# A token table built in setup: its numbers are written out earlier, the own tiles' are gathered first, and the setup's products, mixes and prefills take another order

## Time and profile before

| | us |
|---|---|
| median of 3 runs | 1506.09 |
| lowest, highest | 1505.55, 1506.47 |
| the profiled execution, its own time | 1516.0 |
| its span, first to last instruction | 1514.3 |
| PE busy | 1465.3 (97%) |
| DVE, ACT, POOL busy | 1047.0, 1146.8, 959.1 |
| mean granted clock of PE | 0.997 |

### The profile page before, as it was taken

The page is one execution under the profiler, slowest core; times in us unless marked ns, Lnnn a source line. Parts: engine busy times, 40 slices in busy tenths (PEclk is TensorE's granted clock), DMA queues, the critical chain, the costliest instruction groups (busy, mean ns, idle before and its releaser), DMA issues. The chain is left out here.

```text
span 1514.3 us, 33889 instructions
## 1 busy us (share of the span) xinstructions
PE 1465.3 (97%) x11160; PEld 1339.9 (88%) x11160; DVE 1047.0 (69%) x2811; ACT 1146.8 (76%) x3477; POOL 959.1 (63%) x991
## 2 busy tenths in 40 slices
PE   5789999999999999999999999988999999999999
PEld 2469888888888988889888898877999999999999
DVE  7887788788777887778887787763344333356665
ACT  5589888888888888888888888865555555555555
POOL 7175567888788888788878877664677566510000
PEclk9999999999999999999999999999999999999999
DMA  7324511211211111111111111022244234456665
GB/s 237 132 73 163 164 38 49 69 48 42 60 38 39 55 42 36 35 56 34 36 56 34 37 38 48 26 60 67 69 116 106 70 71 109 120 158 190 189 184 146
DMA packets 171503, 126.48 MB, mean 84 GB/s; under 512 B 30309, under 2 KB 154959, under 8 KB 171330
## 3 DMA queue, kind: packets, MB, share of 16 engines
q1 hardware_dynamic: 153794, 104.15, 23.3%
q0 software_dynamic: 17536, 20.17, 4.8%
HBM read 61.64 MB, written 78.66 MB: 93 GB/s over the span
## 5 line engine op out<-in xcount | busy, mean ns | idle before, releaser
L1129 ACT ACTIVATE expd<-masked,nmax 128x128 f32<-128x128 f32 x1024 | 396.0, 393 | 0.3 <-DVE nmax L1282 0.3
L925 POOL TENSOR_TENSOR prob<-expd,rtotal 128x1024 f32<-128x1024 f32 x128 | 243.5, 1902 | 117.3 <-DVE rtotal L1251 115.8
L1265 DVE COPY_PREDICATED masked<-off_diag,ps_s 128x1024 f32<-128x1024 int32 x128 | 175.0, 1367 | 164.3 <-PE ps_s L1018 164.3
L1062 PE MATMUL ps_o<-u,probT 128*128 128x128 f32 x2048 | 249.0, 275 | 0.0
L1062 PEld LDWEIGHTS ps_o<-u,probT 128*128 128x128 f32 x2048 | 238.9, 191 | 0.0
L1129 ACT ACTIVATION_READ_ACCUMULATOR expd<-masked,nmax 128x1 f32 x1024 | 197.0, 192 | 0.0
L1138 ACT ACTIVATE u<-ps_ut 128x1024 f32<-128x1024 f32 x128 | 131.4, 1026 | 66.3 <-PE ps_ut L1073 66.3
L1227 DVE TENSOR_TENSOR w_lo<-ps_w,w_hi 128x512 fp32r<-128x512 f32 x256 | 164.3, 681 | 0.9 <-ACT w_hi L1167 0.9
L1167 ACT ACTIVATE w_hi<-ps_w 128x512 fp32r<-128x512 f32 x256 | 146.1, 595 | 15.7 <-PE ps_w L1048 9.3
L1158 ACT ACTIVATE probT<-ps_ut 128x1024 f32<-128x1024 f32 x128 | 131.4, 1027 | 33.9 <-PE ps_ut L1030 27.5
L1046 PE MATMUL ps_w<-xT_hi,M_hi 128*128 128x256 f32 x512 | 154.1, 301 | 3.0 <-DVE xT_lo L1221 2.2
(11 more groups left out here) (261 smaller groups left out, 3824.9 us busy)
## 6 DMA issues: line engine op xcount, KB each, us to landing
turned<-x2T SPq DMA_DIRECT2D x32, 256.0 KB, 2.2
answers_sp<-zeros SPq DMA_DIRECT2D x16, 512.0 KB, 4.3
answers_fq<-zeros SPq DMA_DIRECT2D x16, 512.0 KB, 3.8
xT<-turned SPq DMA_DIRECT2D x56, 128.0 KB, 2.3
sh_back<-answers_sp SPq DMA_DIRECT2D x56, 128.0 KB, 2.4
sh_back<-answers_fq SPq DMA_DIRECT2D x56, 128.0 KB, 2.5
out<-res SPq DMA_DIRECT2D x56, 128.0 KB, 2.1
h_sb<-in_L_tok_weight SPq DMA_DIRECT2D x12, 512.0 KB, 5.9
```

The costliest lines, as they stand in the source:

```text
L925: nc.gpsimd.tensor_tensor(prob[k % 2][:, :].rearrange("p (g j) -> p g j", g=H), expd[k % 2][:, :].rearrange("p (g j) -> p g j", g=H), rtot ...
L1062: mm = nc.tensor.matmul(ps_o[:, 0:D], probT[k % 2][:, g * N:(g + 1) * N], u[k % 2][:, g * D:(g + 1) * D], start=(g == 0), stop=(g == H - 1))
L1129: ins = nc.scalar.activation(expd[(k - 1) % 2][:, g * N:(g + 1) * N], masked[(k - 1) % 2][:, g * N:(g + 1) * N], ACT.Exp, bias=nmax[(k - 1 ...
L1265: nc.vector.copy_predicated(masked[k % 2][:, :].rearrange("p (g j) -> p g j", g=H), off_diag[:, :].unsqueeze(1).to_broadcast([P, H, N]), p ...
```

## The change

- DVE writes the plain numbers (not the thousandths) and the flags into `numbers` early, the flags in the middle of `thousandths`, which now runs once over all 98 columns; the thousandths go to `part`. SP writes `kept` right after the small loads, **ahead** of the three weight loads and the rows, after a wait for the numbers and the flags.
- The four number gathers stand on POOL ahead of `head_of`'s masks, and the four row gathers behind them: two after the masks, two after the ten small memsets, all ahead of the mixes.
- The gathered numbers are plain, so DVE makes their thousandths at c == 5 (8 more small operations).
- `turn_b` is made by POOL (8 operations) in place of DVE.
- PE does the first turn and the coefficients at c == 3 (before c == 2), the other turns at 4 and 5, the products from c == 6 on, the last two at c == 12.
- The prefills go from ACT to POOL, right behind the mixes.
- `WARM` goes from 13 to 6.

The diff, cut to its core:

```diff
--- before.py
+++ after.py
@@ -56,7 +56,7 @@
 AHEAD = 2
-WARM = 13
+WARM = 6
 CLEARS = B * N // P // CLEAR_ROWS
...
@@ -296,7 +296,7 @@
-        part = sb("part", [P, 4, VS])
+        part = sb("part", [P, 3, VX])
@@ -378,16 +378,28 @@
...
             made["own"] = link.n
+            link.inc(nc.gpsimd.tensor_scalar(turn_b, row_f[:, :], TURN_HI, 0.0, ALU.mult, ALU.add))
+            link.inc(nc.gpsimd.tensor_scalar(turn_lo, row_f[:, :], TURN_LO, 0.0, ALU.mult, ALU.add))
+            link(nc.gpsimd.tensor_scalar(turn_hi.bitcast(F32R), row_f[:, :], TURN_HI, 0.0, ALU.mult, ALU.add))
+            link(nc.gpsimd.tensor_tensor(turn_b, turn_b, turn_hi, ALU.subtract))
+            link(nc.gpsimd.tensor_tensor(turn_lo, turn_lo, turn_b, ALU.add))
+            link(nc.gpsimd.tensor_tensor(turn_b, turn_hi, turn_lo, ALU.subtract))
+            pool.wait_ge(S["link"], 1)
+            link(nc.gpsimd.tensor_tensor(turn_b, turn_b, is_hi[:, :].to_broadcast([KR, D]), ALU.mult))
+            nc.gpsimd.tensor_tensor(turn_b, turn_b, turn_lo, ALU.add).then_inc(S["turn"], 1)
             def own_number(t):
...
                                              bass.IndirectOffsetOnAxis(ap=ids0[:, t:t + 1], axis=0)).then_inc(S["numbers0"], 16)
-            pool.wait_ge(S["ids0"], 16)
-            for t in range(OWN):
+            def own_row(t):
                 nc.gpsimd.indirect_dma_start(h_sb[:, (VS + t) * D:(VS + t + 1) * D], None, weight,
                                              bass.IndirectOffsetOnAxis(ap=ids0[:, t:t + 1], axis=0)).then_inc(S["rows0"], 16)
+            pool.wait_ge(S["ids0"], 16)
+            pool.wait_ge(S["kept"], 32)
+            for t in range(OWN):
+                own_number(t)
             link.inc(nc.gpsimd.memset(head_of[:, :], 1.0))
...
@@ -404,18 +416,22 @@
...
                                         mix_co[:, c % HC, c // HC, :].unsqueeze(2).to_broadcast([P, H, D]), ALU.mult).then_inc(S["mixed"], 1)
-            pool.wait_ge(S["kept"], 32)
-            for t in range(OWN):
-                own_number(t)
-            pool.wait_ge(S["coef_out"], 2)
-            pool.wait_ge(S["wT_out"], 1)
-            for c in range(2 * HC):
-                mix(c)
+            for t in range(2):
+                own_row(t)
             for t, value in ((C.power, -0.5), (C.ones, 1.0), (C.tri, 1.0), (C.carry, 0.0), (C.chosen, 0.0), (C.var, 1.0)):
...
             made["mv1"] = link.n
+            for t in range(2, OWN):
+                own_row(t)
+            pool.wait_ge(S["coef_out"], 2)
+            pool.wait_ge(S["wT_out"], 1)
+            for c in range(2 * HC):
+                mix(c)
+            for k in range(2):
+                link.inc(nc.gpsimd.tensor_copy(masked[k][:, :].rearrange("p (g j) -> p g j", g=H),
+                                               diag[:, :].unsqueeze(2).to_broadcast([P, H, N])))
             link.inc(nc.gpsimd.iota(C.rank_i[:, :], [[-1, E]], base=E, channel_multiplier=0))
...
@@ -443,14 +459,14 @@
...
                 sp.dma_start(dst, src, allow_slow_non_contiguous=True).then_inc(S["small"], 16)
+            sp.wait_ge(S["numbers"], 2)
+            sp.dma_start(kept[0:P * VR, :].rearrange("(p r) c -> p (r c)", p=P),
+                         numbers[:, 0:VR, :].rearrange("p r c -> p (r c)")).then_inc(S["kept"], 16)
+            sp.dma_start(kept[P * VR:VOCAB, :], numbers[0:REST, VR, :]).then_inc(S["kept"], 16)
             for dst, src in ((wq[:, :], Wq), (wkv[:, :], Wkv),
...
             sp.dma_start(h_sb[:, cols(0)], w_main[:, cols(0)]).then_inc(s_row[0], 16)
-            sp.wait_ge(S["numbers"], 1)
-            sp.dma_start(kept[0:P * VR, :].rearrange("(p r) c -> p (r c)", p=P),
-                         numbers[:, 0:VR, :].rearrange("p r c -> p (r c)")).then_inc(S["kept"], 16)
-            sp.dma_start(kept[P * VR:VOCAB, :], numbers[0:REST, VR, :]).then_inc(S["kept"], 16)
             one = slice((CHUNKS - 1) * CH, VR * D)
...
@@ -499,10 +515,6 @@
...
                 nc.scalar.activation(turns[c % 2][:, 0:w], ps_a[c % 2][:, 0:w], ACT.Copy).then_inc(S["whole"], 1)
-            def prefill(k):
-                nc.scalar.activation(masked[k][:, :].rearrange("p (g j) -> p g j", g=H),
-                                     diag[:, :].unsqueeze(2).to_broadcast([P, H, N]), ACT.Copy).then_inc(S["coef_out"], 1)
             def sines(c):
...
@@ -522,7 +534,7 @@
...
                     rest_of_numbers()
-                if c == 2:
+                if c == 3:
                     act.wait_ge(S["wT"], 1)
...
@@ -532,15 +544,10 @@
...
                     nc.scalar.activation((wkT, wvT)[c - 4][:, :, :].rearrange("p c n -> p (c n)"), ps_t[:, :], ACT.Copy).then_inc(S["wT_out"], 1)
-                if c == 4:
-                    act.wait_ge(S["coef_out"], 2)
-                    prefill(0)
                 if c == 6:
...
                     nc.scalar.activation(numT[:, 12 * P:13 * P], short_rows, ACT.Copy).then_inc(S["numT_out"], 1)
-                if c == CHUNKS - 2:
-                    prefill(1)
-                if c == 9:
+                if c == 10:
                     act.wait_ge(S["M"], 2)
...
@@ -606,73 +613,61 @@
...
             angles(1)
-            pe.wait_ge(S["num_f"], 2)
             for c in range(4, CHUNKS - 1):
...
                 angles(c)
-                if c == 2:
+                if c == 3:
                     turn(0)
                     coefficients()
-                if c in (3, 4):
-                    turn(c - 2)
+                if c in (4, 5):
+                    turn(c - 3)
                 if c == 6:
-                    pe.wait_ge(S["num_f"], 3)
+                    pe.wait_ge(S["num_f"], 2)
                     number_rows(CHUNKS - 1).then_inc(S["numT"], 1)
-                if 5 <= c:
+                for n in {6: (0,), 7: (1,), 8: (2,), 9: (3,), 10: (4,), 11: (5,), 12: (6, 7)}.get(c, ()):
                     for half in range(2):
-                        product((c - 5) // HC, (c - 5) % HC, half)
+                        product(n // HC, n % HC, half)
             pe.wait_ge(S["reduced"], CHUNKS - 1)
...
         def _(dve):
-            link = Chain(dve, sem("s_link"))
-            def thousandths(at):
-                value, q, hi, lo = (part[:, n, at] for n in range(4))
-                link(nc.vector.tensor_copy(value, num_i[:, at]))
+            link = Chain(dve, S["link"])
+            def thousandths(at, flags=False):
+                value, (q, hi, lo) = numbers[:, at, 0], (part[:, n, at] for n in range(3))
                 link(nc.vector.tensor_scalar(q, value, 0.001, None, ALU.mult))
...
                 link(nc.vector.tensor_tensor(hi, hi, lo, ALU.subtract))
+                if flags:
+                    dve.wait_ge(S["isn"], 32)
+                    nc.vector.tensor_copy(numbers[:, 0:VR, 1].bitcast(I32), isn[:, 0:VR]).then_inc(S["numbers"], 1)
+                    nc.vector.tensor_copy(numbers[:, VR:VS, 1].bitcast(I32), rest_isn[:, 0:1]).then_inc(S["numbers"], 1)
                 link(nc.vector.tensor_tensor(lo, q, hi, ALU.subtract))
...
                 link(nc.vector.scalar_tensor_tensor(lo, lo, -1000.0, hi, ALU.mult, ALU.add))
-                link(nc.vector.scalar_tensor_tensor(numbers[:, at, 0], lo, 0.001, q, ALU.mult, ALU.add))
+                link(nc.vector.scalar_tensor_tensor(q, lo, 0.001, q, ALU.mult, ALU.add))
             def halves(chunks, n):
-                src = numbers[:, chunks.start * VC:chunks.start * VC + (chunks.stop - chunks.start) * n, 0].rearrange("p (c r) -> p c r", r=n)
-                for part in (0, 2):
-                    link.inc(nc.vector.tensor_copy(num_hl[:, chunks, 0:n, part], src))
-                link.wait()
-                for part in (0, 2):
-                    ins = nc.vector.tensor_tensor(num_hl[:, chunks, 0:n, part + 1], src, num_hl[:, chunks, 0:n, part].bitcast(F32), ALU.subtract)
-                ins.then_inc(S["num_f"], 1)
+                src = part[:, 0, chunks.start * VC:chunks.start * VC + (chunks.stop - chunks.start) * n].rearrange("p (c r) -> p c r", r=n)
+                high, low = (num_hl[:, chunks, 0:n, k:PARTS:2] for k in range(2))
+                both = src.unsqueeze(3).to_broadcast([P, chunks.stop - chunks.start, n, 2])
+                link(nc.vector.tensor_copy(high, both))
+                nc.vector.tensor_tensor(low, both, high.bitcast(F32), ALU.subtract).then_inc(S["num_f"], 1)
             dve.wait_ge(S["made"], made["own"])
             link.inc(nc.vector.tensor_reduce(is_hi[:, :], own_hi[:, :], X_AXIS, ALU.max))
-            link.inc(nc.vector.tensor_scalar(turn_b, row_f[:, :], TURN_HI, None, ALU.mult))
-            link(nc.vector.tensor_scalar(turn_hi.bitcast(F32R), row_f[:, :], TURN_HI, None, ALU.mult))
-            link(nc.vector.tensor_tensor(turn_b, turn_b, turn_hi, ALU.subtract))
-            link(nc.vector.scalar_tensor_tensor(turn_lo, row_f[:, :], TURN_LO, turn_b, ALU.mult, ALU.add))
-            link(nc.vector.tensor_tensor(turn_b, turn_hi, turn_lo, ALU.subtract))
```

(17 more changed lines are left out.)

## The result

The kernel after takes **1522.46 us** (median of 4 runs, 1521.57 to 1523.46) where the kernel before took 1505.82 beside it (4 runs, 1504.11 to 1506.47): ratio 1.0112 [1.0095, 1.0130], slower by 16.6 us. The forecast, 1510.2, had the sign, and its range ended at 1514.5. The profiled execution of after took 1521.61 us, 1519.9 of them the span.

What follows compares the result with a forecast made beforehand. PE, busy 97%, was taken as the bound, so a shift of setup's barrier shifts the end: 3.5 + 2.0 - 1.4 = 4.1 us later, 1520.1 profiled, carried over to the median as 1510.2; range 1503.5 to 1514.5.

Steps and rivals of the forecast that it cites:

- the last line of the sum: Whole kernel: 1520.1 us profiled, taken as 9.9 above the median and carried over to that as 1510.2.
- the mark: Start of PE's first work behind the barrier ending setup; the sum had that barrier 4.1 us later.
- R: Moment in setup when PE gets the last gathered numbers: 42.1 us before, forecast 45.6, 3.5 later.
- POOL hands over after each instruction: Rival, chance 0.10: at c == 5 DVE's ten small operations each wait one mix, R 37, 1501.6 us.
- Numbers earlier: Start of setup: numbers and flags go out earlier, POOL's number gathers go on at 10.8 us (8.4 to 12.3).
- Masks: POOL in setup: masks behind the four number gathers are done at 18.0 us, against 11.5 before.
- Mixes: POOL in setup: with row gathers ahead, two hit by predicated copies, mixes start at 25.8 us, against 23.9.
- Prefills: POOL behind the mixes: two prefills at 1.0 us each, so POOL is through at 42.7.
- c == 5: DVE's ten small operations wait for POOL's end at 42.7, then take 2.2 us, memset 0.7: R 45.6.
- Products: PE behind R: all eight products follow, one more than before, 1.98 us; the first is slow, 3.27.
- The end: End of setup: six spare products instead of 13 save 1.4 us before the barrier.
- turn_b: Start of setup: made on POOL, ready at about 6.8 us against 5.2, the delay hidden.

Runs made afterwards that it cites:

- after_idle: Kernel after with one small POOL memset, and a wait for its own end, ahead of the first mix: 1518.99 us.
- after_hold: Kernel after with POOL's mixes starting only when the third predicated copy is finished: 1520.56 us.
- before_again: Kernel before, unchanged, run again: five of ten runs at 1503.47 to 1507.09 us, five at 1513.96 to 1516.78; its trace 1503.47.
- before_under_copy: Kernel before with POOL waiting for `reduce(4)`, so that the first mix starts just behind the start of the third predicated copy: 1506.14 us.
- before_idle: Kernel before with one small POOL memset, and a wait for its own end, ahead of the mixes: 1504.62 us, ratio 1.0001.
- before_gap: Kernel before with every mix waiting until the one before it is done: 1505.48 us, ratio 0.9977.
- before_warm6: Kernel before with 6 spare products at the end of setup in place of 13: ratio 1.0023, its trace 1522.44 us.

## Why the prediction was wrong

**The step that failed is the last line of the sum**: "it stands 9.9 above the median of 1506.09, and carried over to that the forecast is 1510.2". Against its own profiled execution the sum was nearly right: 1520.1 forecast, 1521.6 measured. Part of that was luck: the mark came 6.8 us later (64.85 to 71.64), not 4.1, since R moved 6.2 and not 3.5, and 1.2 us came back behind the barrier (1451.2 to 1450.0), where the sum had nothing. But the 9.9 us were no offset that comes with profiling. They were the hold itself, R 42.10 instead of 31.59, absent from most runs of before and, by three traces (18.54 us, 17.93 with 13 spare products, 16.57 without the prefills) and by the times, present in every run of after. A change that makes a chance event certain costs its whole price against the median; I carried the price over as if both kernels paid it.

The numbers were in plain sight: a profiled execution 9.9 us, 0.66%, above runs that agreed within 0.9 us. I wrote the gap down and did not ask what it was.

**The rivals.** "POOL hands over after each instruction" was given 0.10 on the ground that one event in one trace showed no hand-over. It is what before does in its short course (1.63 us for the copy, 1.82 for the small operations). But its price was wrong as well: for after it gave R at 37 and 1501.6, a gain. Where after does take turns, the ten small operations need 15.5 and 15.8 us, not some 10, R is 44.06 and 44.48, and the time 1519.0 and 1520.6 (after_idle, after_hold), still slower than before. None of my rivals put the turns into before and not into after, which is where 1521 comes from.

The Trainium skill ("SBUF — State Buffer", Who interferes with whom) lets the second of two contending operations wait for the first one's end, one instruction. I set that aside for the earlier trace rows. Both are seen: the short course of before, after_hold and after_idle do what the page says, with 1.6 us for the copy and 1.8 for the two-input operations on 128x4 elements; the stream straight behind a gather does not, at 15.58, 16.57 and 18.54. Where they differ the traces decide, and they say that how the stream starts has a part in it.

By my steps, against the trace of after:

1. *Numbers earlier*: first gather 10.8 forecast (8.4 to 12.3), 11.88 measured.
2. *Masks*: 18.0 forecast, 20.12 measured, when the second `affine_select` was through. The copy at 17.71 blocked the first one (1.72 us, the second 0.60), a meeting that I had priced for gathers only. PE waited 2.75 for it; hidden, because the end of this stretch was R.
3. *Mixes*: 25.8 forecast, 26.81 measured, the one late mask and one blocked gather (1.82) in it.
4. *Prefills*: 2.0 forecast for both, 2.02 measured, and they do hold DVE.
5. *c == 5*: R 45.6 forecast, 48.31 measured. I had either the copy through ahead of the mixes, or held with the mixes early; it was issued at 26.26, ahead of a late first mix at 26.81, and was held nonetheless. So POOL's late start and the copy with `reduce(5)` behind POOL's end both counted, 2.7 us more.
6. *Products*: one more behind R, right. The first was slow (3.36 us, 3.3 forecast).
7. *The end*: 1.2 saved in the traces (1.4 forecast), though WARM = 6 alone made before no faster.
8. *turn_b*: ready at 7.17 (6.8 forecast), hidden, right.

Steps 2, 3 and 5 add up to most of the difference between 45.6 and 48.31. They made R 2.7 us too early; the ten that put the result outside the range are the carry-over.

## What to carry to other kernels

Where the profiled execution and the other times of the same kernel differ by more than those times do among themselves, find out what the extra time is before any sum is carried over: a stall in the trace may be missing from most runs, and then a change may remove nothing or make it certain. Do not issue a gather on POOL directly ahead of a stream of POOL operations that contend with DVE; here a memset of 0.14 us with its own wait, or 0.29 us of idling, was enough, each time with the first mix falling under a running copy, so look in the trace whether it worked. And count DVE's operations that fall beside such a stream rather than their size: each may cost a whole POOL instruction, so chains of tiny ones belong ahead of it or behind it.

## What the runs showed that I had not expected

- DVE's predicated copy is held over a **whole stream** of POOL instructions (8 or 10 of them: 15.58, 16.57, 18.54 us) when the first of them follows a gather within 0.03 us and no gaps are put between them, and for one instruction or none (1.30 to 3.62) otherwise. Idling of 0.28 us or more, a memset of 0.14 us, or gaps between the mixes ended it. That is shown in both kernels. **One rival stands**: in all four gapless kernels in which a copy got its turn (before_again, before_under_copy, before_idle, after_idle) the first mix had itself waited for a running copy (2.34 to 2.97 us in place of 1.9), and wherever the copy was held it had not (1.90 to 1.91). Theory W, that POOL's having waited once is what brings the turns, fits these as well as G. The kernel that would part them, a gapless stream behind an idle POOL with no copy in flight and a predicated copy coming later, was not run. Why the hardware does so is open under either. Only a predicated copy has been seen held in this way. Whether another operation would be was not tried in a stream behind a gather, and after_hold, the one stream that neither followed a gather nor waited for a copy, met small operations only.
- The copy need not be the late one: at 26.26 in after it stood ahead of the first mix, and under a gather.
- Two orders 0.3 us apart (gather at 16.81 or 17.14, copy at 17.0) decide 10 us of a 1504 us kernel. The traces agree that this parts its runs (gather first in before_again, before_gap and before_idle; copy first in that of the prediction, in before_warm6 and before_under_copy, the last made short by its wait); only three of these are of a kernel with the stream unedited, and for the many times without a trace it is inferred from their two groups.
- Blocking runs the other way as well: a POOL gather issued just behind the start of a predicated copy takes 1.8 to 2.0 us instead of 0.95, and an `affine_select` on 8x512 elements 1.72 instead of 0.60.
- Operations on 128x4 elements took 1.82 us each beside POOL's mixes, eleven times their 0.16 to 0.17 alone. With gaps between the mixes, it was every second one, 1.75 us.
